# Second expert mixture: tokens sorted by their chosen experts, against all experts for all tokens

## The reference

```python
x = x + ao @ wo
h = _rmsnorm(x, ln2_w)
logits = h @ router_w
probs = jax.nn.softmax(logits, axis=-1)
topv, topi = jax.lax.top_k(probs, TOPK)          # TOPK = 2, E = 8, M = 448
topv = topv / jnp.sum(topv, axis=-1, keepdims=True)
weights = jnp.sum(jax.nn.one_hot(topi, E, dtype=h.dtype) * topv[..., None], axis=-2)
gate = jnp.einsum('bsd,edm->bsem', h, w_gate)
up = jnp.einsum('bsd,edm->bsem', h, w_up)
act = jax.nn.silu(gate) * up * weights[..., None]
moe = jnp.einsum('bsem,emd->bsd', act, w_down)
return x + moe
```

## Time and profile before

| | |
|---|---|
| median of three runs | 1034.48 us |
| profiled execution, device time | 1034.8 us |
| its span, first to last instruction | 1033.0 us |
| PE busy | 959.3 us, 93% |
| DVE, ACT, POOL busy | 739.8, 615.9, 195.3 us |
| end of attention to first router matmul of the second mixture | 572.08 to 581.09 us |
| routing | 581.09 to 592.12 us |
| its expert loop | 592.12 to 734.15 us |

### The profile page before, as it was taken

The page is one execution under the profiler, slowest core; times in us unless marked ns, Lnnn a source line. Parts: engine busy times, 40 slices in busy tenths (PEclk is TensorE's granted clock), DMA queues, the critical chain, the costliest instruction groups (busy, mean ns, idle before and its releaser), DMA issues.

```text
span 1033.0 us, 15853 instructions
## 1 busy us (share of the span) xinstructions
PE 959.3 (93%) x5322; PEld 607.2 (59%) x5345; DVE 739.8 (72%) x1184; ACT 615.9 (60%) x1042; POOL 195.3 (19%) x150
## 2 busy tenths in 40 slices
PE   9899889998898889898998799999898999999997
PEld 5566546665355433465355467777445777777775
DVE  4566537777787485686587677776627988888897
ACT  5366435555555453665655365555556888888887
POOL 0111042321000000000100622422300334333340
PEclk9999999999999998999999999999989999999999
DMA  8000000110000000000000001001003988887882
GB/s 332 0 1 0 1 15 32 46 54 1 1 2 1 1 1 0 1 2 1 1 3 1 27 28 53 27 27 42 21 21 89 227 224 230 225 222 217 225 217 80
DMA packets 22241, 69.65 MB, mean 67 GB/s; under 512 B 3856, under 2 KB 5136, under 8 KB 21808
## 3 DMA queue, kind: packets, MB, share of 16 engines
q1 hardware_dynamic: 22192, 68.99, 23.5%
HBM read 67.79 MB, written 1.18 MB: 67 GB/s over the span
## 4 chain that ended last, share of the span: by engine, by line
PE 69%; DVE 18%; ACT 9%; issue 3%; DMA 1%; DVEq 0%; SPq 0%; POOL 0%; another core or an unknown queue 0%; ACTq 0%; POOLq 0%
PE ps L656 14%; PE ps L658 12%; PE ps L657 12%; PE ps L505 3%; PE ps L497 3%; PE ps L522 2%; PE ps L199 2%; PE ps L516 2%; DVE parts L690 2%; ACT arena L1409 2%; DVE arena L629 2%; ACT rstd L217 2%; ACT rstd L220 1%; DVE arena L633 1%; PE ps L1107 1%
## 5 line engine op out<-in xcount | busy, mean ns | idle before, releaser
L656 PE MATMUL ps<-parts 128*128 128x512 f32 (+2 forms) x608 | 258.1, 424 | 9.3 <-DVE parts L870 4.1
L658 PE MATMUL ps<-parts 128*128 128x512 f32 (+2 forms) x608 | 239.0, 393 | 0.0
L657 PE MATMUL ps<-parts 128*128 128x512 f32 (+2 forms) x608 | 238.9, 393 | 0.0
L686 ACT ACTIVATE parts<-ps 128x512 fp32r<-128x512 f32 (+1 forms) x256 | 153.2, 598 | 118.8 <-DVE ps L875 71.2
L690 DVE TENSOR_TENSOR parts<-ps,parts 128x512 fp32r<-128x512 f32 (+1 forms) x256 | 174.8, 683 | 1.1 <-ACT parts L686 0.9
L656 PEld LDWEIGHTS ps<-parts 128*128 128x128 f32 (+2 forms) x608 | 112.4, 185 | 82.5 <-DVE ps L1959 32.0
L674 POOL TENSOR_TENSOR parts<-ring,zeros 128x1024 fp32r<-128x1024 f32 (+4 forms) x52 | 73.2, 1421 | 404.1 <-PE ps L658 267.1
L658 PEld LDWEIGHTS ps<-parts 128*128 128x128 f32 (+2 forms) x608 | 112.4, 185 | 27.8
L1959 DVE TENSOR_TENSOR ps<-ps,arena 128x512 f32<-128x512 f32 x156 | 109.2, 700 | 25.5 <-DVE parts L690 14.5
L657 PEld LDWEIGHTS ps<-parts 128*128 128x128 f32 (+2 forms) x608 | 113.0, 186 | 18.5 <-issue 0.5
L875 DVE TENSOR_TENSOR ps<-arena,ps 112x512 f32<-112x512 f32 (+1 forms) x96 | 66.8, 696 | 54.3 <-PE ps L658 52.0
(11 more groups left out here) (356 smaller groups left out, 1218.0 us busy)
## 6 DMA issues: line engine op xcount, KB each, us to landing
arena<-m_comb SPq DMA_DIRECT2D x156, 256.0 KB, 4.1
ring<-m_in SPq DMA_DIRECT2D x20, 512.0 KB, 5.1
ring<-m_up_in SPq DMA_DIRECT2D x8, 448.0 KB, 3.5
pack<-pack_in SPq DMA_DIRECT2D x1, 2058.5 KB, 10.6
ring<-m_up_in SPq DMA_DIRECT2D x8, 256.0 KB, 2.6
ring<-m_down_in SPq DMA_DIRECT2D x8, 224.0 KB, 3.5
pack<-pack_in SPq DMA_DIRECT2D x1, 1149.5 KB, 12.8
pack<-pack_in SPq DMA_DIRECT2D x1, 1096.0 KB, 14.8
```

The costliest lines, as they stand in the source:

```text
L656: nc.tensor.matmul(dst, w_high, x_high, start=start, stop=False, skip_group_check=True)
L657: nc.tensor.matmul(dst, w_high, x_low, start=False, stop=False, skip_group_check=True)
L658: return nc.tensor.matmul(dst, w_low, x_high, start=False, stop=stop, skip_group_check=True)
L686: nc.scalar.activation(m_hh[0:rows, p], ps[0:rows, src, :], ACT.Copy).then_inc(R(t, "_hh"), 1)
```

## The change

The second mixture no longer runs every expert over every token. The first one and the third keep their code.

1. **Counting.** Routing finds the two largest logits as before, and makes a mask of 0 and 1 (token, expert). Nine small bf16 matmuls with a triangle and a square of ones (`upto`) give each token its running number within each expert, and each expert its total. DVE rounds totals up to blocks of 128, sums them up, and has for each token two slot numbers (`s_idx`), and for each of 23 blocks its expert (`s_off`, as a column offset). 2048 pairs and at most 7 partly filled blocks more make NB = 2 * 1024 / 128 + 8 - 1 = 23.
2. **Scatter.** PE transposes the input to rows of tokens; ACT copies them twice into `s_rows`, each with its destination number as the 129th element. POOL issues 16 indirect DMAs (128 rows of 516 bytes each), which write each row to its slot in a DRAM tensor `slots_x`. That tensor was filled earlier, by a copy from DRAM, with zero rows whose 129th element points at unused rows.
3. **Fetch.** SP waits for all 16, and loads the slots back in four pieces (1, 3, 8 and 11 blocks).
4. **Blocks.** PE reads 23 registers from `s_off`, issues 70 matmuls on zeros (`FILL_SCATTER`), and runs the 23 blocks, written out without a loop. A block is: one transpose of the input, gate and up as one full fp32 matmul each (128 tokens stationary, 448 weight columns moving, picked by register), four transposes of the hidden values, four down matmuls. ACT copies the input and the result and does silu; DVE multiplies gate by up and copies the transposed hidden values. Weights are plain fp32: all eight experts (5.5 MB) are loaded by four DMAs at the end of the attention, and POOL splits nothing.
5. **Back.** Behind each block POOL issues one indirect DMA that writes its 128 result rows to `slots_y`, each to the row that its 129th element names. SP waits for all 23, loads both results of every token (4 DMAs of 256 KB), and PE multiplies them with 16 diagonal matrices of the routing weights, which sums, weights and transposes them back into banks 0 and 1. Ahead of it PE has 30 matmuls on zeros (`FILL_TABLE`).

Some buffers, constants and semaphores are added; SP has one small load more (`upto`) at the start, and the first loads for the last mixture stand behind the fetch instead of behind the splits.

```diff
+NB = 2 * T // P + E - 1
+M2_COLS = 2 * M2_HID + M2_CH * P
+ROW = P + 1
+LOADS = (0, 1, 4, 12, NB)
+FILL_SCATTER, FILL_TABLE = 70, 30
...
+        def sorted_load(sp):
+            sp.dma_start(slots_x, empty_in).then_inc(R("m2", "_load1"), 16)
+            sp.wait_ge(S("f2_attn"), 2)
+            for e in range(0, E, 2):
+                sp.dma_start(s_w[:, e:e + 2, :], m2_in[e:e + 2].rearrange("e p n -> p e n")).then_inc(R("m2", "_load0"), 16)
+            sp.wait_ge(S("s_scattered"), 16 * 2 * B)
+            for n in range(len(LOADS) - 1):
+                lo, hi = LOADS[n], LOADS[n + 1]
+                sp.dma_start(s_xs[:, lo:hi, :], slots_x[1 + P * lo:1 + P * hi, :].rearrange("(j s) c -> s j c", s=P)).then_inc(R("m2", f"_c{n}"), 16)
+
+        def sorted_tables(sp):
+            sp.wait_ge(S("s_out"), 16 * NB)
+            for p in range(2):
+                for k in range(2):
+                    lo = T * k + HALF * p
+                    sp.dma_start(s_yab[:, k, HB * p:HB * (p + 1), :],
+                                 slots_y[lo:lo + HALF, :].rearrange("(b t) f -> t b f", t=P)).then_inc(R("slots", ("_z", "_p")[p]), 16)
+
+        def sorted_gpsimd(pool):
...
+            for k in range(2):
+                for b in range(B):
+                    nc.gpsimd.indirect_dma_start(slots_x, bass.IndirectOffsetOnAxis(ap=s_idx[:, k, b:b + 1], axis=0),
+                                                 s_rows[:, k, b, :], None).then_inc(S("s_scattered"), 16)
+            for j in range(NB):
+                waits(pool, "m2")("_xwh", j + 1)
+                nc.gpsimd.indirect_dma_start(slots_y, bass.IndirectOffsetOnAxis(ap=s_to[:, j, P:P + 1], axis=0),
+                                             s_xs[:, j, 0:P], None).then_inc(S("s_out"), 16)
+
+        def sorted_tensor(pe):
+            mm = nc.tensor.matmul
...
+            fill(14, 6)
+            waits(pe, "m2")("_wh", 2)
+            mm(ps[:, 3, 0:(B + 1) * E], upto[:, 0, :], s_mask[:, :], start=True, stop=False, skip_group_check=True)
+            for k in range(1, B + 1):
+                ins = mm(ps[:, 3, k * E:(B + 1) * E], upto[:, 1, :], s_mask[:, 0:(B + 1 - k) * E], start=False, stop=(k == B), skip_group_check=True)
+            ins.then_inc(R("m2", "_wturned"), 1)
+            waits(pe, "m2")("_wT", 1)
+            at = [pe.value_load(s_off[0:1, j:j + 1], min_val=0, max_val=(E - 1) * M2_COLS) for j in range(NB)]
+            fill(FILL_SCATTER, 6)
+            waits(pe, "m2")("_load0", 16 * E // 2)
...
+            def gate_up(j):
+                for k, (name, freed) in enumerate((("_gate", "_silu"), ("_up", "_hid"))):
+                    if j >= 2:
+                        waits(pe, "m2")(freed, j - 1)
+                    mm(ps[:, 2 * k + j % 2, 0:M2_HID], s_xT[:, j % 2, :], s_wflat[:, bass.ds(at[j] + k * M2_HID, M2_HID)],
+                       start=True, stop=True).then_inc(R("m2", name), 1)
+
+            def turn_h(j):
...
+                for c in range(M2_CH):
+                    ins = nc.tensor.transpose(ps[0:M2_ROWS, 5 + j % 2, c * P:(c + 1) * P], s_h[:, j % 2, c * M2_ROWS:(c + 1) * M2_ROWS], ident)
+                ins.then_inc(R("m2", "_hh"), 1)
+
+            def down(j):
...
+                for c in range(M2_CH):
+                    ins = mm(ps[:, 7, 0:P], s_hT[0:M2_ROWS, j % 2, c * P:(c + 1) * P],
+                             s_wflat[0:M2_ROWS, bass.ds(at[j] + 2 * M2_HID + c * P, P)], start=(c == 0), stop=(c == M2_CH - 1))
+                ins.then_inc(R("m2", "_xw"), 1)
+
+            turn_x(0)
+            for j in range(NB + 2):
+                if j < NB:
+                    waits(pe, "m2")("_spread", j + 1)
+                    if j + 1 < NB:
+                        turn_x(j + 1)
+                    gate_up(j)
+                if 1 <= j <= NB:
+                    turn_h(j - 1)
+                if j >= 2:
+                    down(j - 2)
+            fill(FILL_TABLE, 6)
+            waits(pe, "m2")("_pad", 1)
+            for p in range(2):
+                waits(pe, "slots")(("_z", "_p")[p], 32)
+                for b in range(HB * p, HB * (p + 1)):
+                    for k in range(2):
+                        ins = mm(ps[:, p, (b % HB) * P:(b % HB + 1) * P], s_yab[:, k, b, :], s_diag[k][:, b, :], start=(k == 0), stop=(k == 1),
+                                 skip_group_check=True)
+                ins.then_inc(S("y_ready"), 1)
...
+        def sorted_vector(dve, link):
...
+            link(V.tensor_scalar(s_nb, ps[:, 3, B * E:(B + 1) * E], P / 2 - 0.5, 1.0 / P, ALU.add, ALU.mult))
+            link(V.tensor_scalar(s_nb, s_nb, ROUND, ROUND, ALU.add, ALU.subtract))
+            link(V.tensor_tensor_scan(s_end, ones8[:, 0, 0:1].to_broadcast([P, E]), s_nb, 0.0, ALU.mult, ALU.add))
...
+            V.tensor_copy(s_idx[:, 1, :], s_mx).then_inc(R("m2", "_xh"), 1)
+            V.tensor_tensor(s_idx[:, 0, :], s_sum, s_mx, ALU.subtract).then_inc(R("m2", "_xh"), 1)
...
+            for k in range(2):
+                for b in range(B):
+                    ins = V.tensor_scalar(s_diag[k][:, b, :], ident, s_wk[:, k, b:b + 1], None, ALU.mult)
+            ins.then_inc(R("m2", "_pad"), 1)
...
-            mix_load(sp, "m2", m2_up_in, m2_down_in, M2_CH, M2_ROWS)
-            waits(sp, "m2")("_split", E)
+            sorted_load(sp)
...
-            route_tensor(pe, "m2", m_x2, 14)
-            mix_tensor(pe, "m2", M2_CH, M2_ROWS)
+            sorted_tensor(pe)
...
-            mix_gpsimd(pool, "m2", m_x2, M2_CH, M2_ROWS, lambda: pool.wait_ge(S("f2_attn"), 2))
+            sorted_gpsimd(pool)
```

More of the change, by code:

```diff
@@ L16 @@
 U8 = mybir.dt.uint8
+U32 = mybir.dt.uint32
+I32 = mybir.dt.int32
 ALU = mybir.AluOpType
@@ L1364, in _ @@
                 ins.then_inc(R("m3", "_wturned"), 1)
-            pe.wait_ge(S("m3_rows"), 1)
+            waits(pe, "slots")("_turned", 1)
             spread(0, 0)
@@ L1566, in _ @@
             waits(act, "m3")("_wturned", 1)
-            A_(half(t_rows, 0), bank(4), ACT.Copy).then_inc(S("m3_rows"), 1)
-            A_(half(t_last, 0)[0:NE - P, :], ps[0:NE - P, 6, :], ACT.Copy).then_inc(S("m3_rows"), 1)
+            A_(half(t_rows, 0), bank(4), ACT.Copy).then_inc(R("slots", "_turned"), 1)
+            A_(half(t_last, 0)[0:NE - P, :], ps[0:NE - P, 6, :], ACT.Copy).then_inc(R("slots", "_turned"), 1)
             def m3_group(i, lead, final):
@@ L1972, in _ @@
             waits(dve, "m3")("_wT", 2)
-            dve.wait_ge(S("m3_rows"), 2)
+            waits(dve, "slots")("_turned", 2)
             m3_hidden(0, 0, 0, LEAD)
@@ L2139 @@
     m3 = m3.transpose(0, 3, 1, 2, 4).reshape(2 * GROUPS, P, 1024)
+    down2 = i["L2_ffn_w_down"].reshape(E, M2_CH, M2_ROWS, P).transpose(0, 2, 1, 3).reshape(E, M2_ROWS, M2_CH * P)
+    down2 = np.concatenate([down2, np.zeros((E, P - M2_ROWS, M2_CH * P), np.float32)], axis=1)
+    m2 = np.concatenate([i["L2_ffn_w_gate"], i["L2_ffn_w_up"], down2], axis=2)
+    upto = np.stack([np.triu(np.ones((P, P))), np.ones((P, P))], axis=1)
+    empty = np.zeros((SLOT_ROWS, ROW), np.float32)
+    empty[:, P] = (2 * T + np.arange(SLOT_ROWS)).astype(np.int32).view(np.float32)
     w13, w2 = i["L0_ffn_w13"], i["L0_ffn_w2"]
```

185 lines of the change are left out of this document (161 added, 24 removed).

## The result

| | before | after |
|---|---|---|
| median | 1036.03 us (4 runs, 1031.73 to 1037.62) | 1000.31 us (4 runs, 997.96 to 1002.50) |
| profiled execution | 1034.8 us | 1000.4 us |
| ratio after/before | | 0.9661, 95% interval 0.9622 to 0.9700 |

The change is faster by 3.4%.

What follows compares the result with a forecast made beforehand. The second mixture was taken as bound by PE's column count alone. Its stage terms put y_ready at 713.9 instead of 734.15, -20.3 us; 1034.8 became 1014.5, less 0.3 to the median: 1014.2 us, range 1001 to 1036.

Steps and rivals of the forecast that it cites:

- PE's block at 3.8 us: Expert blocks: PE needs 3.63 us plus 0.17 each, bounds 3.63 and 4.2; 23 blocks take 87.4 us.
- The surcharge for register addresses: Expert blocks: extra instructions for register addresses add 0.04 us per 128-column product, 0.17 us per block.
- The register loads, priced at 0.35 us: Before the blocks: PE's 23 register loads take 8.0 us, costing nothing up to 0.47 us each.
- PE's register loads are dear: Rival, chance 0.13: from 0.47 us each, loads delay the first block; 1017 at 0.6 us, 1033 at 1.28.
- the 3.0 us in front of the routing: Ahead of routing: without POOL's split, DVE's two operations writing `m_x2` finish 3.0 us earlier.
- My own sign for this term: Ahead of routing: `m_x2`'s two DVE operations near 0.75 us each and router products near 578, else the term fails.
- the scatter's pitch: Scatter: POOL issues 16 indirect DMAs at 1.36 us each, 21.8 us; over 2 us would prove the forecast wrong.
- Consumers: Expert blocks: ACT under 1.8 us, DVE 1.4 and POOL's DMA 1.36 per block all hide behind PE.
- The way back: After the blocks: last DMA, landing, loads and eight products take 10.5 us to `y_ready`, bounds 8 and 14.
- The weights were in SBUF in time: Before the blocks: 5.5 MB of weights loaded by 592, or 603 at half rate, covered by the scatter.
- The rule against it: Scatter: DVE's writing of 16 diagonal matrices could lock POOL out of issuing DMAs for 4 us, giving 1018.
- My floor: Whole kernel: quicker scatter, blocks at 3.63 us and 8 us for the way back give 1000 to 1002.

Runs made afterwards that it cites:

- e9: Kernel after the change with 24 instead of 70 filling matmuls behind the register loads; 992.29 us, ratio 0.9614.
- e4: Kernel after the change without the 23 register loads, every block taking expert 0's weights at a fixed address; 995.09 us, ratio 0.9634.
- e1: Kernel after the change with each block's five transposes issued as ordinary fp32 products with the identity; 1011.61 us, ratio 0.9802.
- e5: Kernel before the change, with POOL's first weight split of the second mixture held back until `m_x2` is written; 1033.72 us, ratio 1.0021.
- e12: Kernel after the change with 24 instead of 70 fills, and POOL's first splits for the last mixture moved behind the whole next layer; 988.38 us, ratio 0.9552.
- e6: Kernel after the change without the 30 filling matmuls (`FILL_TABLE`) behind the blocks; 1005.71 us, ratio 0.9720.
- e8: Kernel after with fills between register loads, fewer before counting, and POOL's first last-mixture splits held until the third layer's recurrence ends; 992.40 us, ratio 0.9609.
- e3: Kernel after the change with three fills behind each register load and ten behind the last, replacing the 70 behind all; 995.97 us, ratio 0.9625.
- e11: Kernel after the change without the 70 fills, and with eight more indirect DMAs ahead of the scatter; 1003.21 us (one run).

## Why the prediction was right and wrong

All from the common point, in us; the forecast's own numbers less 574.65.

| | forecast | measured |
|---|---|---|
| `m_x2` written | +3.4 | +3.37 |
| first router product | +3.4 | +4.75 |
| `s_idx`; block table | +13.9; +14.7 | +13.0; +13.8 |
| scatter, 16 DMAs | 21.8 | 20.3 |
| PE ready (loads and fills done) | +37.8 | +47.3 |
| data there | +40.6 | about +37.5 (e9, e4) |
| first block | +40.6 | +47.3 |
| 23 blocks, with the first turn | 88.2 | 69.8 |
| last product to `y_ready` | 10.5 | 11.1 |

The rows of the first block, of the 23 blocks and of the way to `y_ready` differ by +6.7, -18.4 and +0.6: the stage is 11.1 us better than forecast, and 3.2 more lie ahead of it. With the 20.3 forecast that is 34.6, for 34.4 measured.

**The step that failed: PE's block at 3.8 us.** "5 transposes and 4 down products of 128 columns, 9 x 0.236". The pace of the earlier trace rows is that of full fp32 products, with two records each. A transpose has one, and takes 0.11 us: 5 x 0.126 x 23 = 14.5 us too many. The right row stood in the trace of the kernel before, and was not among mine: L505, eight transposes in 1.09 us, x8 and not x16. The surcharge for register addresses, 0.17 us a block, was 3.9 more; e4 shows that there is none. The four down products took 0.89 us and not 0.94, another 1.2. Against these 19.6 us stands 1.2 that I had too little for the first and last blocks, where one stage of the block waits for another: 18.4 are left. e1 put back 12.2 us of the 14.5, by making the same five of one block full products, at 0.22 us each and not at my 0.236. Gate and up at 1.50 us were exact.

**The register loads, priced at 0.35 us, took 0.67.** This was the rival "PE's register loads are dear": its threshold of 0.47 us was passed, and it took place, with the sign and mechanism given: the first block stood straight behind the filling matmuls, and these ran partly at half clock. PE was ready 9.5 us later than forecast: 7.4 more for the loads (15.44 against 8.0) and 2.9 more for the fills (18.0 from their start to the first block, against 15.1), less 0.8 by which the block table came earlier. The Trainium skill ("DMA: Bandwidth & Descriptors", Latency and other measured facts) had about 600 ns as the floor for such a load; the trace agrees with 0.67, and I should have given the higher value the weight. By that page's figure the first block would have started at an estimated +43.6.

**Half right: the 3.0 us in front of the routing.** DVE's part came to within 0.1, and e5 showed the cause. But I took PE as free for the router's products and left out its 19 filling matmuls, which held them to +4.75; of the 3.0 us, 1.7 reached PE. My own sign for this term, router products near 578, thus failed by 1.35 us. It did no harm to the sum, because the eight transposes took 1.07 us and not 1.9 (the same wrong row), and DVE's chain was quicker: `s_idx` still came 0.9 us early.

**Right:** the scatter's pitch was 1.27 us against my 1.36; data came 3.1 us earlier than forecast. Consumers (DVE, ACT, POOL's output DMA) hid behind PE: PE is busy 68.97 of 70 us. The way back cost 11.1 against 10.5. The weights were in SBUF in time.

**The rule against it.** DVE wrote its diagonals from 586.69 on, for 3.25 us. POOL's first DMA, 1.17 us, was over by then; the second and third took 1.02 and 1.07 us beside them, the others 0.96: 0.17 us in sum, not 4. The Trainium skill ("SBUF — State Buffer", The "DVE blocks DMA" trap) says that POOL can't write descriptors while DVE holds the port that they share; here that is at most a delay of 0.1 us per DMA. Whether DVE's operations were of the kind that the page means, no run here shows.

**What the range missed.** The register loads, at 0.67 us, lay inside their bounds of 0.12 and 1.28; the block, at 2.95 us, lay far below its own of 3.63 to 4.2. My floor (block 3.63) rested on the same wrong row as the forecast, so the range had no room on that side. That the median lies only 0.7 us below the range is luck: the two errors went in opposite directions. The block's alone, 18.4 us, would have brought the forecast to 996.

What stays open: why the granted clock rose about 3 us earlier in e12, e1 and e6 than in e9 and the kernel after, and with it how many fills are best on the average.

## What to carry to other kernels

Price an instruction by a row of the same kind, and look first at the number of records per instruction: here x1 for an fp32 transpose and x2 for an fp32 product was a factor of two on five of nine instructions. When work on one engine is there to bridge a wait (the filling matmuls), count from where its own engine is free, not from where the wait begins: 70 fills behind 15 us of register loads started the blocks 9.8 us late and saved them 2.3; 24 fills brought the first block forward by the 9.8 us and, in one of three profiled executions, kept the saving. In the medians this is 8 us, within the noise of the ratios. When POOL slows DVE, moving POOL's work can pick another victim (e5 gained nothing, e8 less than half of what its scans gave back): find a place where DVE idles, and look at the step behind it as well, and at what PE is doing when the data come.

## What the runs showed of the hardware

- An fp32 transpose of 128x128 costs 0.11 us on PE at the full clock (kernel after), the same as an ordinary product 0.22 us (e1).
- A register load from SBUF on PE takes 0.67 us; with 23 in a row PE did nothing else for 15.44 us, and the granted clock of that stretch was 0.53. Matmuls put in between are partly covered (e3: 24.4 us for 15.4 and 17.1).
- An indirect DMA of 128 rows of 516 bytes holds POOL for 0.96 us and comes every 1.26 to 1.27 us (kernel after, e11).
- DVE's SBUF-to-SBUF operations were 3 to 6 times slower beside POOL's tensor operations: four scans 6.55 us against 1.36, L1898 2.50 against 0.75, L730 1.29 against 0.23. Beside POOL's indirect DMAs the 16 diagonals followed each other every 0.20 us (3.25 us for all).
- Matmuls whose weight or input address comes from a register kept the pace of those with a fixed one (2.95 us a block in both).
